# An attention and feed-forward kernel on one core: early subtractions moved from GpSimd to VectorE, a new order of the early stages, and weight loads issued once half 0's x has arrived

## The chip, the core and the metric

The program runs on one core of a Trainium2 chip. The core has TensorE (matmul; PE, its weight loads PEld), VectorE (DVE), ScalarE (ACT), GpSimd (POOL), and SyncE (SP), which here only issues transfers. Each engine works through its own instructions in program order, and engines wait for one another with semaphores. The metric is the device time of one execution in microseconds (us).

## The reference

For 1,024 tokens (32 sequences of 32, 256 features): x is conditioned by a matrix and a bias chosen for each sequence, goes through causal attention with 16 heads, is added back, and then passes a gated layer with low-rank adapters chosen for each sequence, a second gated layer with a Hadamard transform, and a last addition.

```
cond = einsum("bct,bcd->bdt", x, w[subject]) + bias[subject]
q, k, v = split(cond @ W_qkv + b_qkv)
att = softmax(where(causal, q @ k.T / 16, -inf))
x = x + (att @ v) @ W_out + b_out
h = silu(lora(x, Wg, Ag, Bg)) * lora(x, Wu, Au, Bu)
y = lora(h, Wd, Ad, Bd)
x = x + fwht(silu(y @ W1.T) * (y @ W3.T)) @ W2.T
```

## The kernel before

The tokens are handled as two halves of 512 columns, `s` = 0 and 1, and the features in two blocks of 128, `c` or `m` = 0 and 1. To keep float32 precision each operand of a large matmul is a sum of two parts, a hi part (rounded copy, made on ScalarE) and a lo part (the rest, a subtraction), and a product takes three matmuls (hi by hi, lo by hi, hi by lo).

A weight batch `n` of 128 x 512 values is loaded by SyncE into `raw[n % 3]` (`load_weights`), copied on ScalarE into `w_hi` (`split_weights`) and subtracted on GpSimd into `w_lo` (`weights_lo`). So batch n + 3 can be loaded only once `w_lo` of batch n exists. The first batches are W_K = 0, W_Q = 1, W_V = 2, W_OUT = 3, W_GU = 4 and on.

The early stages, in the words of the functions: VectorE picks each slot's conditioning matrix (`condition_product`, `condition_sum`, `condition_blocks`); TensorE multiplies x with it (`conditioned`) and adds the bias (`conditioned_bias`, from a table `fbias` that `condition_bias` makes); ScalarE and VectorE split the result (`conditioned_hi`, `conditioned_lo`). Then come `key` and `query` on TensorE, copied out with a bias by `keys` (half 0: heads 0 and 1 on ScalarE, heads 2 and 3 on VectorE, which waits for ScalarE's) and `queries`; `scores` on TensorE; for each of four score tiles of a half `maxima`, `less_maxima`, `sums`, `inverses` on VectorE, `exps` on ScalarE, `normalised` on GpSimd, `turn` (a transpose) on VectorE, `spread_slots` on ScalarE and `spread_first` on GpSimd; then `v` and `values` on TensorE. The result is gathered by `even_heads` (ScalarE) and `odd_heads` (VectorE) and split by `attention_hi` (ScalarE) and `attention_lo` (VectorE) for the output projection `project`. The residual sum and the gated layers follow.

All orders are written out by hand: each engine's block is a list of calls. SyncE's and ScalarE's transfers go into one queue each, and both queues use the same 16 DMA engines. At the start ScalarE's queue loads the index and x of half 0 (`x_slot[0]`, line 850), SyncE's the constants, three weight batches, x of half 1, `matrix`, `a_in_raw` and `resid` (lines 397 to 435), and then W_OUT and W_GU.

Of the kernel before, what the change touches and what calls it, by code (L numbers as in the profile page):

```python
# [37 lines left out]
ALU = mybir.AluOpType  # L38
# [3 lines left out]
P = 128  # L42
# [64 lines left out]
KEEP_WARM = 4  # L107
# [58 lines left out]
def build(nc, index, first, x_slots, w_stream, matrices, w2_t, x_feat, out):  # L166
    with ExitStack() as ctx:
# [3 lines left out]
        def sem(name):  # L171
            return ctx.enter_context(nc.semaphore(name))
# [106 lines left out]
        w_hi_made = sem("w_hi_made")  # L279
        w_lo_made = sem("w_lo_made")  # L280
# [115 lines left out]
        def _(sp):  # L396
# [33 lines left out]
            for n in range(STAGES):  # L430
                load_weights(n)
# [44 lines left out]
        def _(pe):  # L476
# [66 lines left out]
            def projected(name, n, s, m):  # L543
                w = weights(n)
                ps = claim(name, s, m)
                for c in range(DC):
                    wait_conditioned(s, c)
                    last = both([ps], unit(w, m * DC + c), rows(act_hi, act_lo, c, [s]), c == 0, c == DC - 1)
                full(last[0], name, s, m)

# [297 lines left out]
        def _(act):  # L848
# [220 lines left out]
        def _(dve):  # L1069
# [7 lines left out]
            dve.tensor_copy(idx_row, index_i[:, NG:NG + B]).then_inc(setup, 1)  # L1077
# [7 lines left out]
            def batch_onehots():  # L1085
                dve.wait_ge(setup, 2)
                dve.wait_ge(row_made, 2)
                dve.tensor_scalar(onehot_n[0:2 * LO_ROW, :], idx_row[0:2 * LO_ROW], adapter_row[0:2 * LO_ROW, :], None,
                                  ALU.is_equal).then_inc(onehot_n_made, 1)

            def condition_sum(s):
                dve.wait_ge(prod_cond, s + 1)
                dve.tensor_reduce(cond_sel[:, s * GROUPS:(s + 1) * GROUPS], cond_prod[s], AX.X, ALU.add)\
                   .then_inc(sel_made, 1)

# [154 lines left out]
            batch_onehots()  # L1250
# [15 lines left out]
            keys(0, 1, 2, 3)  # L1266
# [100 lines left out]
        def _(pool):  # L1367
            def weights_lo(n):
                at = n % PLACES * COLS
                pool.wait_ge(w_hi_made, n + 1)  # L1370
                pool.tensor_tensor(w_lo[:, at:at + COLS], raw[:, n % STAGES, :], f32(w_hi[:, at:at + COLS]),  # L1371
                                   ALU.subtract).then_inc(w_lo_made, 1)

# [7 lines left out]
                               float(LO_ROW), None, ALU.subtract).then_inc(row_made, 1)  # L1381
            pool.wait_ge(row_made, 2)
            pool.tensor_tensor(k_bias[:, :, :], const[:, B_K:B_K + DC].unsqueeze(2).to_broadcast([P, DC, 4]),
                               four.unsqueeze(1).to_broadcast([P, DC, 4]), ALU.mult).then_inc(k_bias_made, 1)
            pool.wait_ge(k_bias_made, 1)
# [70 lines left out]
            weights_lo(W_GU)  # L1456
# [3 lines left out]
            spread_first(0, 1, 2, 3)  # L1460
            gather_in(1, 3)
# [129 lines left out]
```

## Time and profile before

| | |
|---|---|
| median of 3 runs | 213.04 us (212.9 to 213.07) |
| the profiled execution | 212.89 us, of which its profile spans 211.1 us |
| PE busy | 205.1 us (97%) |
| DVE, ACT, POOL busy | 93.2, 94.6, 110.4 us |
| DMA | 16.70 MB, mean 79 GB/s |

Times in the profile count from the span's start. The 1.8 us between span and time lie outside the profile. PE's busy time is modelled; what an engine waited for stands in brackets in a timeline row.

### The profile page before, as it was taken

The page shows a single profiled execution, that of the slowest core. Times are in us where ns is not written, and L with a number is a line of the kernel's source. Part 1 is how long each engine was busy: PE and PEld are TensorE (multiplying, and loading weights), DVE is VectorE, ACT ScalarE, POOL GpSimd, SP SyncE. Part 2 cuts the span into 40 slices and gives each one's busy share as a digit, 9 for nine tenths or more (in the row PEclk, how much of TensorE's full clock was granted, in tenths as well). Part 3 has the DMA queues.
Part 4 walks back from the last instruction along what each step waited for, and adds up shares of the span by engine and source line. Part 5 has one row for each costly group of instructions (what it writes and reads, how often), then busy time and mean ns, then how long its engine had stood idle before and what let it go on. Part 6 is the DMA issues. An engine that isn't in the chain of part 4 may idle for free.

```text
span 211.1 us, 5890 instructions
## 1 busy us (share of the span) xinstructions
PE 205.1 (97%) x2361; PEld 163.1 (77%) x2362; DVE 93.2 (44%) x166; ACT 94.6 (45%) x165; POOL 110.4 (52%) x126
## 2 busy tenths in 40 slices
PE   7899999899999999999999999999999999999994
PEld 2567788578777878788788788888888888888894
DVE  3786997895549883020220300068822222220211
ACT  3377898576846043261350361314566664420000
POOL 4596787159846040936742449002699999440000
PEclk9999999999999999999999999999999999999999
DMA  6960055725430470031210460201021000000211
GB/s 148 397 216 5 6 154 156 202 56 159 132 102 0 115 212 31 17 98 25 58 29 23 112 248 11 91 0 50 3 51 50 0 3 0 0 0 3 99 50 50
DMA packets 16266, 16.70 MB, mean 79 GB/s; under 512 B 1776, under 2 KB 13040, under 8 KB 15984
## 3 DMA queue, kind: packets, MB, share of 16 engines
q1 hardware_dynamic: 15952, 15.78, 24.3%
q10 hardware_dynamic: 288, 0.54, 1.1%
q8 instruction: 19, 0.31, 0.6%
q14 instruction: 7, 0.06, 0.1%
HBM read 15.27 MB, written 1.05 MB: 77 GB/s over the span
## 4 chain that ended last, share of the span: by engine, by line
PE 89%; DMA 3%; DVE 3%; ACT 2%; POOL 1%; issue 1%; SPq 0%; POOLq 0%; ACTq 0%; DVEq 0%
PE bank L500 25%; PE bank L502 23%; PE bank L504 23%; PE bank L672 8%; DMA raw<-w_stream 3%; PE bank L712 2%; PE bank L589 2%; PE bank L615 2%; POOL w_lo L1371 1%; DVE aux_lo L1174 1%; PE bank L568 1%; ACT aux_hi L924 1%; PE bank L569 1%; PE bank L570 1%; DVE resid L1182 1%
## 5 line engine op out<-in xcount | busy, mean ns | idle before, releaser
L1429 POOL TENSOR_TENSOR h_lo<-tmp_b,h_hi 128x512 fp32r<-128x512 f32 x32 | 42.6, 1352 | 43.5 <-ACT h_hi L938 43.5
L500 PE MATMUL bank<-act_hi,w_hi 128*128 128x512 f32 x144 | 52.9, 403 | 0.4 <-POOL w_lo L1371 0.2
L502 PE MATMUL bank<-act_lo,w_hi 128*128 128x512 f32 x144 | 51.0, 390 | 0.0
L504 PE MATMUL bank<-act_hi,w_lo 128*128 128x512 f32 x144 | 50.9, 390 | 0.0
L1244 DVE TENSOR_TENSOR tmp_b<-bank,tmp_a 128x512 f32<-128x512 f32 x32 | 20.8, 685 | 62.5 <-ACT tmp_a L945 36.4
L1371 POOL TENSOR_TENSOR w_lo<-raw,w_hi 128x512 fp32r<-128x512 f32 x24 | 31.4, 1315 | 23.6 <-ACT w_hi L868 23.6
L500 PEld LDWEIGHTS bank<-act_hi,w_hi 128*128 128x128 f32 x144 | 27.0, 188 | 8.4 <-issue 1.9
L945 ACT ACTIVATE tmp_a<-bank 128x512 f32<-128x512 f32 x32 | 17.3, 592 | 32.6 <-PE bank L672 28.4
L504 PEld LDWEIGHTS bank<-act_hi,w_lo 128*128 128x128 f32 x144 | 27.0, 188 | 5.8
L502 PEld LDWEIGHTS bank<-act_lo,w_hi 128*128 128x128 f32 x144 | 27.1, 188 | 5.1
L938 ACT ACTIVATE h_hi<-tmp_b 128x512 fp32r<-128x512 f32 x32 | 19.7, 632 | 20.2 <-DVE tmp_b L1244 20.2
L500 PE MATMUL bank<-h_hi,w_hi 128*128 128x512 f32 (+1 forms) x72 | 22.8, 371 | 0.0
L502 PE MATMUL bank<-h_lo,w_hi 128*128 128x512 f32 (+1 forms) x72 | 22.5, 366 | 0.0
L504 PE MATMUL bank<-h_hi,w_lo 128*128 128x512 f32 (+1 forms) x72 | 22.4, 366 | 0.0
L868 ACT ACTIVATE w_hi<-raw 128x512 fp32r<-128x512 f32 x24 | 14.4, 619 | 7.7 <-DMA raw<-w_stream 7.7
L672 PE MATMUL bank<-z_slots,b_own 64*64 64x128 f32 x512 | 15.8, 272 | 0.0
L502 PEld LDWEIGHTS bank<-h_lo,w_hi 128*128 128x128 f32 x72 | 13.6, 189 | 2.3
L504 PEld LDWEIGHTS bank<-h_hi,w_lo 128*128 128x128 f32 x72 | 13.6, 189 | 2.2
L500 PEld LDWEIGHTS bank<-h_hi,w_hi 128*128 128x128 f32 x72 | 13.3, 189 | 2.5 <-issue 0.3
L672 PEld LDWEIGHTS bank<-z_slots,b_own 64*64 64x64 f32 x512 | 13.9, 132 | 1.5 <-issue 1.1
L1344 DVE TENSOR_TENSOR act_lo<-bank,act_hi 128x512 fp32r<-128x512 f32 x4 | 2.6, 686 | 19.3 <-ACT act_hi L1055 19.3
L1416 POOL TENSOR_TENSOR prob<-prob,row_inv 128x512 f32<-128x512 f32 x8 | 8.4, 1051 | 5.1 <-DVE row_inv L1157 5.0
(97 smaller groups left out, 245.7 us busy)
## 6 DMA issues: line engine op xcount, KB each, us to landing
raw<-w_stream SPq DMA_DIRECT2D x24, 256.0 KB, 4.1
b_own<-w_stream SPq DMA_DIRECT2D x32, 128.0 KB, 3.0
resid<-x_feat SPq DMA_DIRECT2D x1, 1024.0 KB, 9.0
tmp_a<-w_t SPq DMA_DIRECT2D x1, 1024.0 KB, 5.1
out_feat<-tmp_b SPq DMA_DIRECT2D x3, 256.0 KB, 2.1
k_x<-x_slots ACTq DMA_DIRECT2D x1, 512.0 KB, 5.1
k_x<-x_slots SPq DMA_DIRECT2D x1, 512.0 KB, 7.2
a_down_raw<-w_stream SPq DMA_DIRECT2D x1, 512.0 KB, 4.0
```

What stands on the lines that cost most here:

```text
L500: pe.matmul(ps[:, :], w[0], x_hi, start=start, stop=False)
L502: pe.matmul(ps[:, :], w[0], x_lo, start=False, stop=False)
L504: last.append(pe.matmul(ps[:, :], w[1], x_hi, start=False, stop=stop))
L589: last = pe.matmul(tiles[i][32 * j:32 * j + 32, g * 4 * T:(g + 1) * 4 * T], q_t[s][q, c, b * T:(b + 1) * T], k_x[s][q, c, b], start=False, ...
L672: ins = pe.matmul(tile(name, s, m)[features, at:at + P], weight(name, s, m, rows_, q)[:, features], slots(name, s, rows_, q).rearrange("p ...
L868: act.activation(w_hi[:, at:at + COLS], raw[:, n % STAGES, :], ACT.Copy)\
L938: act.activation(dst, tmp_b[:, ORDINAL[name, s, m] % 4, :], ACT.Copy).then_inc(prod_hi_made, 1)
L945: free(act.activation(tmp_a[:, n % 4, :], tile(name, s, m)[:, :], ACT.Silu), name, s, m)
L1244: free(dve.tensor_tensor(tmp_b[:, ORDINAL[name, s, m] % 4, :], tile(name, s, m)[:, :], tmp_a[:, silus % 4, :], ALU.mult), name, s, m)
L1371: pool.tensor_tensor(w_lo[:, at:at + COLS], raw[:, n % STAGES, :], f32(w_hi[:, at:at + COLS]), ALU.subtract).then_inc(w_lo_made, 1)
L1416: pool.tensor_tensor(prob[s][:, i], prob[s][:, i], row_inv[:, s, i, :].unsqueeze(2) .to_broadcast([P, 16, T]), ALU.mult).then_inc(normed, 1)
L1429: pool.tensor_tensor(lo, tmp_b[:, n % 4, :], f32(hi), ALU.subtract).then_inc(prod_split, 1)
```

## The change

- `weights_lo` of W_K and W_Q, and `condition_bias(0)`, move from GpSimd to VectorE; `condition_product(1)`, the row of indices and `onehot_n` move from VectorE to GpSimd.
- TensorE drops four filler matmuls (KEEP_WARM), and its first key and query have functions that wait for the lo parts only where each is read. `key(0, 1)` now stands ahead of half 1's conditioning, and `scores(0, 1)` ahead of `key(1, 1)`.
- ScalarE does `keys(0, 1, 0, 1)` ahead of `conditioned_hi(1, ...)`, VectorE does `keys(0, 1, 2, 3)` ahead of `conditioned_lo(1, ...)`.
- GpSimd does `weights_lo(W_GU)` behind half 0's last `spread_first`.
- SyncE issues only W_K at once. It waits until half 0's x has arrived, and then issues W_Q, W_V and all that was behind them.

```
-KEEP_WARM = 4
@@ block.sync
-            for n in range(STAGES):
-                load_weights(n)
+            load_weights(W_K)
+            sp.wait_ge(x_loaded[0], 16)
+            load_weights(W_Q)
+            load_weights(W_V)
             sp.dma_start(x_slot[1], x_slots[:, GROUPS:2 * GROUPS, :]).then_inc(x_loaded[1], 16)
@@ block.tensor
+            def first_key(s, m):
+                ps = claim("k", s, m)
+                for c in range(DC):
+                    at = slice(W_K % PLACES * COLS + (m * DC + c) * P, W_K % PLACES * COLS + (m * DC + c + 1) * P)
+                    wait_read(pe, "xc", s, c)
+                    if c == 0:
+                        pe.wait_ge(w_hi_made, W_K + 1)
+                    pe.matmul(ps[:, :], w_hi[:, at], act_hi[:, c, half(s)], start=c == 0, stop=False)
+                    if c == 0:
+                        pe.wait_ge(w_lo_made, W_K + 1)
+                    pe.matmul(ps[:, :], w_lo[:, at], act_hi[:, c, half(s)], start=False, stop=False)
+                    wait_read(pe, "xd", s, c)
+                    last = pe.matmul(ps[:, :], w_hi[:, at], act_lo[:, c, half(s)], start=False, stop=c == DC - 1)
+                full(last, "k", s, m)
+            def first_query(s, m):
...
+                pe.wait_ge(w_hi_made, W_Q + 1)
...
+                pe.wait_ge(w_lo_made, W_Q + 1)
...
-            for _ in range(KEEP_WARM):
-                pe.matmul(tile("k", 0, 0)[:, :], warm[:, 0:P], warm[:, :], start=True, stop=True)
-            key(0, 0)
-            query(0, 0)
+            first_key(0, 0)
+            first_query(0, 0)
+            key(0, 1)
             conditioned(1, 0)
             conditioned(1, 1)
             conditioned_bias(1, 0)
             conditioned_bias(1, 1)
-            key(0, 1)
             scores(0, 0)
+            query(0, 1)
             key(1, 0)
-            query(0, 1)
+            scores(0, 1)
             key(1, 1)
-            scores(0, 1)
@@ block.scalar
             split_weights(W_OUT)
+            keys(0, 1, 0, 1)
             conditioned_hi(1, 0)
             conditioned_hi(1, 1)
             split_weights(W_GU)
-            keys(0, 1, 0, 1)
+            queries(0, 1)
             exps(0, 0)
             keys(1, 0, 0, 1)
-            queries(0, 1)
@@ block.vector
-            batch_onehots()
             condition_product(0)
             condition_sum(0)
             condition_blocks(0)
-            condition_product(1)
+            condition_bias(0)
+            weights_lo(W_K)
             conditioned_lo(0, 0)
             conditioned_lo(0, 1)
-            identity_rows()
+            weights_lo(W_Q)
             condition_sum(1)
             condition_blocks(1)
+            identity_rows()
+            keys(0, 0, 2, 3)
             row_masks()
-            keys(0, 0, 2, 3)
+            keys(0, 1, 2, 3)
             conditioned_lo(1, 0)
             conditioned_lo(1, 1)
             maxima(0, 0)
             less_maxima(0, 0)
-            keys(0, 1, 2, 3)
             sums(0, 0)
@@ block.gpsimd
-            pool.wait_ge(index_loaded, 16)
-            condition_bias(0)
-            pool.wait_ge(blk_made, 1)
-            weights_lo(W_K)
-            weights_lo(W_Q)
+            pool.wait_ge(w_lo_made, W_K + 1)
+            condition_product(1)
+            pool.wait_ge(fbias_made, 1)
             condition_bias(1)
...
-            weights_lo(W_GU)
             normalised(0, 1)
             spread_first(0, 0)
             normalised(0, 2, 3)
             spread_first(0, 1, 2, 3)
+            weights_lo(W_GU)
             gather_in(1, 3)
             normalised(1, 0)
```

SyncE's first transfers before, with what each waits for (`raw` is a weight batch, `k_x` from `x_slots` is half 1's x):

```order
1 L397 DMA const<-first 128x350
2 L398 DMA fs_rows<-first 8x32
3 L404 DMA raw<-w_stream 128x512 x3
4 L432 DMA k_x<-x_slots 128x1024
7 L435 DMA resid<-x_feat 128x2048
8 L404 DMA raw<-w_stream 128x512 [waits w_lo_made,index_loaded]
```

and in the changed kernel:

```order
3 L404 DMA raw<-w_stream 128x512
4 L404 DMA raw<-w_stream 128x512 [waits x_loaded0]
5 L404 DMA raw<-w_stream 128x512
6 L434 DMA k_x<-x_slots 128x1024
9 L437 DMA resid<-x_feat 128x2048
10 L404 DMA raw<-w_stream 128x512 [waits w_lo_made,index_loaded]
```

The wait stands ahead of the second weight batch, and everything down to W_OUT's load (row 10) is queued behind it.

ScalarE's early instructions before (row 12 is the hi part of W_OUT, row 13 half 1's `conditioned_hi`, row 15 `keys(0, 1, 0, 1)`):

```order
11 L856 ACTIVATE ident_bf<-ident_rows 128x128
12 L868 ACTIVATE w_hi<-raw 128x512
13 L874 ACTIVATE act_hi<-bank 128x512 x2
14 L868 ACTIVATE w_hi<-raw 128x512
15 L889 ACTIVATE k_x<-bank,k_bias,const 128x16x32 x2
16 L905 ACTIVATE prob<-prob 128x512
```

and in the changed kernel:

```order
11 L884 ACTIVATE ident_bf<-ident_rows 128x128
12 L896 ACTIVATE w_hi<-raw 128x512
13 L917 ACTIVATE k_x<-bank,k_bias,const 128x16x32 x2
14 L902 ACTIVATE act_hi<-bank 128x512 x2
15 L896 ACTIVATE w_hi<-raw 128x512
16 L910 ACTIVATE q_t<-bank,const 128x512
17 L933 ACTIVATE prob<-prob 128x512
```

W_OUT's hi part keeps its place; the two key copies now come directly behind it, ahead of half 1's hi parts.

VectorE's instructions before, from half 1's blocks to the first row sums (`k_x` from `bank` are the `keys`, `act_lo` is `conditioned_lo`):

```order
12 L1099 TENSOR_TENSOR prob<-cond_sel,const 128x256
15 L1132 TENSOR_SCALAR k_x<-bank,const,k_bias 128x16x32 x2
16 L1109 TENSOR_TENSOR act_lo<-bank,act_hi 128x512 x2
17 L1140 TENSOR_REDUCE row_max<-bank 128x16
18 L1146 TENSOR_TENSOR prob<-bank,row_max 128x512
19 L1132 TENSOR_SCALAR k_x<-bank,const,k_bias 128x16x32 x2
20 L1152 TENSOR_REDUCE row_sum<-prob 128x16
```

and in the changed kernel:

```order
11 L1134 TENSOR_TENSOR prob<-cond_sel,const 128x256
13 L1167 TENSOR_SCALAR k_x<-bank,const,k_bias 128x16x32 x2
16 L1167 TENSOR_SCALAR k_x<-bank,const,k_bias 128x16x32 x2
17 L1144 TENSOR_TENSOR act_lo<-bank,act_hi 128x512 x2
18 L1175 TENSOR_REDUCE row_max<-bank 128x16
19 L1181 TENSOR_TENSOR prob<-bank,row_max 128x512
20 L1187 TENSOR_REDUCE row_sum<-prob 128x16
```

The second pair of key copies moved from between `less_maxima(0, 0)` and `sums(0, 0)` to ahead of half 1's lo parts.

## Rows read from the trace of the kernel before

**Rows 1.** The page's head, and the granted clock in 40 slices.

```profile
span 211.1 us, 5890 instructions
...
PEclk9999999999999999999999999999999999999999
```

**Rows 2.** The chain that ended last: start us, us, what.

```profile
33.31 1.05 PE bank L615 x60
34.38 0.84 ACT q_t L918 x2
...
36.62 1.58 DVE aux_lo L1174
...
40.73 0.47 PE bank L500
```

**Rows 3.** DMA issues by size: KB each, median us from issue to landing.

```profile
k_x<-x_slots ACTq DMA_DIRECT2D x1, 512.0 KB, 5.1
...
a_down_raw<-w_stream SPq DMA_DIRECT2D x1, 512.0 KB, 4.0
```

**Rows 4.** Landing of L404's loads issued at 2.0, 9.8, 130.4 and 131.7 us.

```profile
L404 SPq DMA_DIRECT2D raw<-w_stream x1: 427/427/427, 2.0 to 2.0; - x1
DMA to landing us min/median/max: 6.2/6.2/6.2
...
L404 SPq DMA_DIRECT2D raw<-w_stream x1: 327/327/327, 9.8 to 9.8; - x1
DMA to landing us min/median/max: 4.6/4.6/4.6
...
DMA to landing us min/median/max: 2.7/2.7/2.7
...
DMA to landing us min/median/max: 5.0/5.0/5.0
```

**Rows 5.** Timeline: start us, us, engine, line, operation, [idle before <-releaser].

```profile
1.19 0.46 ACTq L850 DMA_DIRECT2D k_x<-x_slots  x1
...
12.55 0.99 DVE L1099 TENSOR_TENSOR prob<-cond_sel,const 128x256 f32<-128x256 f32 x1
...
14.99 0.62 ACT L868 ACTIVATE w_hi<-raw 128x512 fp32r<-128x512 f32 x1
...
16.94 1.29 DVE L1109 TENSOR_TENSOR act_lo<-bank,act_hi 128x512 fp32r<-128x512 f32 x2 [1.65 <-ACT act_hi L874]
...
17.66 1.43 ACT L889 ACTIVATE k_x<-bank,k_bias,const 128x512 f32<-128x512 f32 x2
...
19.43 0.69 DVE L1146 TENSOR_TENSOR prob<-bank,row_max 128x512 f32<-128x512 f32 x1
20.04 1.52 DVE L1132 TENSOR_SCALAR k_x<-bank,const,k_bias 128x512 f32<-128x512 f32 x2
20.15 0.63 ACT L905 ACTIVATE prob<-prob 128x512 f32<-128x512 f32 x1 [1.07 <-DVE prob L1146]
...
21.48 0.68 DVE L1152 TENSOR_REDUCE row_sum<-prob 128x16 f32<-128x512 f32 x1
```

**Rows 6.** Timeline of half 0's softmax, the same columns.

```profile
25.62 0.68 DVE L1146 TENSOR_TENSOR prob<-bank,row_max 128x512 f32<-128x512 f32 x1
...
26.65 0.62 ACT L905 ACTIVATE prob<-prob 128x512 f32<-128x512 f32 x1
...
33.05 0.75 ACT L911 ACTIVATE k_x<-k_x,const 128x512 f32<-128x512 f32 x1
```

**Rows 7.** Timeline of GpSimd and VectorE around the attention split.

```profile
24.94 1.31 POOL L1371 TENSOR_TENSOR w_lo<-raw,w_hi 128x512 fp32r<-128x512 f32 x1
...
31.23 1.04 POOL L1422 TENSOR_TENSOR k_x<-k_x,const 128x512 f32<-128x512 f32 x1
...
36.61 1.05 POOL L1416 TENSOR_TENSOR prob<-prob,row_inv 128x512 f32<-128x512 f32 x1 [0.98 <-DVE row_inv L1157]
...
39.84 0.75 DVE L1174 SCALAR_TENSOR_TENSOR aux_lo<-q_t,const,aux_hi 128x512 fp32r<-128x512 f32 x1 [0.25 <-ACT aux_hi L924]
```

More of the change, by code:

```diff
@@ L279, in build @@
         w_hi_made = sem("w_hi_made")
+        idx_row_made = sem("idx_row_made")
         w_lo_made = sem("w_lo_made")
@@ L549, in projected @@
                 full(last[0], name, s, m)
+            def first_key(s, m):
[13 more added lines that the diff above has]
+            def first_query(s, m):
+                ps = claim("q", s, m)
+                at = [slice(W_Q % PLACES * COLS + (m * DC + c) * P, W_Q % PLACES * COLS + (m * DC + c + 1) * P)
+                      for c in range(DC)]
+                pe.wait_ge(w_hi_made, W_Q + 1)
+                for c in range(DC):
+                    pe.matmul(ps[:, :], w_hi[:, at[c]], act_hi[:, c, half(s)], start=c == 0, stop=False)
+                    pe.matmul(ps[:, :], w_hi[:, at[c]], act_lo[:, c, half(s)], start=False, stop=False)
+                pe.wait_ge(w_lo_made, W_Q + 1)
+                for c in range(DC):
+                    last = pe.matmul(ps[:, :], w_lo[:, at[c]], act_hi[:, c, half(s)], start=False, stop=c == DC - 1)
+                full(last, "q", s, m)
             def query(s, m):
@@ L1094, in condition_sum, with condition_bias, weights_lo @@
                    .then_inc(sel_made, 1)
+            def condition_bias(s):
+                b = slice(s * BH, (s + 1) * BH)
+                dve.wait_ge(onehot_n_made, 1)
+                dve.wait_ge(fs_split, 4)
+                dve.tensor_tensor(fbias[:, b], onehot_n[0:BIAS_ROWS, b].unsqueeze(2).to_broadcast([BIAS_ROWS, BH, T]),
+                                  f32(fs_both[:, :]).unsqueeze(1).to_broadcast([BIAS_ROWS, BH, T]), ALU.mult)\
+                   .then_inc(fbias_made, 1)
+            def weights_lo(n):
+                at = n % PLACES * COLS
+                dve.wait_ge(w_hi_made, n + 1)
+                dve.tensor_tensor(w_lo[:, at:at + COLS], raw[:, n % STAGES, :], f32(w_hi[:, at:at + COLS]),
+                                  ALU.subtract).then_inc(w_lo_made, 1)
             def condition_blocks(s):
@@ L1369, in weights_lo @@
                 at = n % PLACES * COLS
+                pool.wait_ge(w_lo_made, n)
                 pool.wait_ge(w_hi_made, n + 1)
@@ L1372, in weights_lo, with condition_product @@
                                    ALU.subtract).then_inc(w_lo_made, 1)
+            def condition_product(s):
+                pool.wait_ge(index_loaded, 16)
+                pool.wait_ge(setup, 1)
+                pool.wait_ge(const_loaded, 16)
+                pool.tensor_tensor(cond_prod[s], cond_all.unsqueeze(1).to_broadcast([P, GROUPS, T, N]),
+                                   onehot_slot[:, s * GROUPS:(s + 1) * GROUPS, :].unsqueeze(2)
+                                   .to_broadcast([P, GROUPS, T, N]), ALU.mult).then_inc(prod_cond, 1)
             pool.memset(f32(ones[:, :]), 1.0).then_inc(ones_made, 1)
@@ L1381, in _ @@
                                float(LO_ROW), None, ALU.subtract).then_inc(row_made, 1)
+            pool.wait_ge(index_loaded, 16)
             pool.wait_ge(row_made, 2)
-            pool.tensor_tensor(k_bias[:, :, :], const[:, B_K:B_K + DC].unsqueeze(2).to_broadcast([P, DC, 4]),
-                               four.unsqueeze(1).to_broadcast([P, DC, 4]), ALU.mult).then_inc(k_bias_made, 1)
-            pool.wait_ge(k_bias_made, 1)
+            pool.tensor_copy(idx_row, index_i[:, NG:NG + B]).then_inc(idx_row_made, 1)
+            pool.wait_ge(idx_row_made, 1)
+            pool.tensor_scalar(onehot_n[0:2 * LO_ROW, :], idx_row[0:2 * LO_ROW], adapter_row[0:2 * LO_ROW, :], None,
+                               ALU.is_equal).then_inc(onehot_n_made, 1)
+            pool.wait_ge(onehot_n_made, 1)
             pool.tensor_copy(fs_both[0:N, :], const[0:N, C_FSIDE:C_FSIDE + T]).then_inc(fs_split, 1)
@@ L1438, in fold_raw_lo @@
                     pool.tensor_tensor(lo, tmp_a[:, j, :], f32(hi), ALU.subtract).then_inc(w2_raw_split, 1)
[L1440 to L1444 removed]
+            pool.wait_ge(fs_split, 4)
+            pool.tensor_tensor(k_bias[:, :, :], const[:, B_K:B_K + DC].unsqueeze(2).to_broadcast([P, DC, 4]),
+                               four.unsqueeze(1).to_broadcast([P, DC, 4]), ALU.mult).then_inc(k_bias_made, 1)
+            pool.wait_ge(w_lo_made, W_K + 1)
+            condition_product(1)
+            pool.wait_ge(fbias_made, 1)
             condition_bias(1)
```

6 lines of the change are left out of this document (removed).

## The prediction

> **What bounds the kernel now.** I read the chain of waits first. From 44 us on it is TensorE alone, one matmul behind the other, so a microsecond won or lost ahead of that point is one in the end time, and nothing behind it is touched by the change. Ahead of it the chain runs over TensorE until the attention output of half 0 at 33.31 us ends, then over ScalarE (34.38 us) and VectorE's `attention_lo` (36.62 us) to the projection at 40.73 us [rows 2]. So two questions decide: when does ScalarE start `even_heads(0, 0)` (34.38 us now; I call this moment E), and how long is the way from E to the projection (6.35 us now)?
>
> E has two masters now. One is TensorE's `values(0, 0)`, which ends at 34.36 us. The other is ScalarE itself: the timeline shows it without a gap from `exps(0, 2)` at 26.65 us to the end of `spread_slots(0, 3)` at 33.05 + 0.75 = 33.80 us [rows 6]. That is only 0.58 us ahead of E. `exps(0, 2)` needs `less_maxima(0, 2)`, which ends at 25.62 + 0.68 = 26.30 us, 0.35 us earlier; I use 0.3 us of it as slack, since a handover costs some 0.05 us. VectorE's softmax work is in turn packed from `sums(0, 0)` at 21.48 us on, one instruction about every 0.6 us with no wait. So TensorE alone being early gives at most 0.58 us. More needs VectorE's `sums(0, 0)` to come earlier, and if that comes later, the loss goes through.
>
> **The change, part by part.**
>
> The loads. Today x of half 0 is issued at 1.19 us and lands 5.1 us later, at 6.3 us [rows 3, 5]; W_Q is issued at 2.0 us and lands 6.2 us later, at 8.2 us; W_OUT is issued at 9.8 us and lands at 14.4 us [rows 4]. These are one unbroken stream: from W_Q's landing to W_OUT's are 6.2 us, for 2,688 KB. ScalarE reads W_OUT at 14.99 us [rows 5], so it has 0.6 us to spare. In the changed kernel the queue runs empty after W_K, and starts again when x is there. When x lands is unknown: not before a 512 KB load with the queue to itself, 4.0 us [rows 3], so 5.2 us; not after today's 6.3 us. I take 5.7 us, since two smaller loads still run beside it. W_Q then takes between 2.7 us, as a lone weight load at 130.4 us did, and 5.0 us, as another lone one at 131.7 us did [rows 4]. I take 3.3 us, nearer the quick one, for most of the 4.0 us of a lone 512 KB load would go to half of it as well [rows 3]. The rest of the stream follows as before, 6.2 us. So W_OUT lands at L = 5.7 + 0.05 + 3.3 + 6.2 = 15.25 us (bounds: 5.2 + 2.7 gives 14.15 us, 6.3 + 5.0 gives 17.55 us). That is 0.85 us later than today. Half 1's x, `matrix` and `a_in_raw` come later by as much; they lie ahead of `resid` in the stream and are needed at 13 us and later, so I cost them at nothing. If that cover is gone, half 1's conditioning slips by the excess, which ScalarE's wait for W_OUT (below) hides up to about 2 us. `resid` is needed only behind the projection.
>
> The Trainium skill, DMA: Bandwidth & Descriptors, Anatomy of one DMA, gives a transfer a fixed cost of about 2.0 us and then bytes over 436 GB/s; by that estimate the 2.75 MB from W_Q to W_OUT take 2.0 + 6.3 = 8.3 us, and L would be 14.05 us, for which the wait below vanishes (the second case among the rivals). It was fitted to GpSimd's transfers, and the trace's lone 5.0 us load is far above its 2.6 us.
>
> ScalarE. Its order puts W_OUT's hi part ahead of `keys(0, 1, 0, 1)` and of half 1's hi parts. It would be ready for it at about 14.1 us: VectorE's `weights_lo(W_Q)` ends near 11.8 us (estimate: the second `conditioned_lo` some 0.5 us earlier than today, then 0.65 us, and as much again if GpSimd's `condition_product(1)` holds it up), then `condition_sum(1)` (1.2 us), blocks (0.99 us today, of which some 0.65 us are a stall beside GpSimd [rows 5]), `identity_rows` (0.4 us) and ScalarE's own copy. All that the change wins before that moment (the bias table and the two lo parts on VectorE at about 0.7 us instead of 1.05 and 1.3 us on GpSimd, the dropped filler, the first key and query some 1.2 to 1.5 us earlier) ends in this wait of 15.25 - 14.1 = 1.15 us. I cost it at nothing, because the cover is a transfer. This is the step that I think matters most.
>
> From L the way to `sums(0, 0)` is a chain of rows. The hi part's pitch is 0.55 us, `keys(0, 1, 0, 1)` take 1.43 us: L + 2.0. VectorE's `keys(0, 1, 2, 3)` wait for them, now ahead of half 1's lo parts, and take 1.45 us to the next instruction (20.04 to 21.48 us): L + 3.5. The two lo parts take 1.2 us at their pitch (1.29 us with the tail): L + 4.7. Then `maxima(0, 0)`, 0.73 us: L + 5.45. From `less_maxima` to the start of `exps` are 0.72 us (19.43 to 20.15), and `exps` take 0.63 us: `sums(0, 0)` at L + 6.8 [rows 5]. At L = 15.25 this is 22.05 us, against 21.48 us now: VectorE is 0.57 us late, although the keys no longer stand in between. The exponent's wait, which the keys filled before, is now idle.
>
> E. `less_maxima(0, 2)` slips by 0.57 us and `exps(0, 2)` by 0.57 - 0.3 = 0.27 us; ScalarE's packed stretch ends at 33.80 + 0.27 = 34.07 us. GpSimd's `spread_first(0, 1)`, which ends at 31.23 + 1.04 = 32.27 us now [rows 7], slips to 32.84 us; `values(0, 0)` take 1.05 us behind it and end at 33.9 us, for TensorE is there about 0.9 us earlier than today. So E = 34.07 us, 0.31 us earlier. As a rule, E = L + 18.8.
>
> From E to the projection. `attention_lo(0, 0)` takes 1.58 us at 36.62 us, and its twin 0.75 us at 39.84 us. The first began 0.01 us behind GpSimd's `normalised(1, 0)`, 36.61 us, which lasts 1.05 us: it stood still until that one had ended [rows 2, 7]. In the changed kernel `weights_lo(W_GU)`, 1.31 us, stands between GpSimd's last `spread_first` and `normalised(1, 0)`. GpSimd starts that `spread_first` at E, ends it at E + 1.1, and is in `weights_lo(W_GU)` until E + 2.4. `attention_lo(0, 0)` is due at E + 2.25, waits 0.15 us, and ends near E + 3.1 instead of E + 3.8. The next step also needs `even_heads(0, 2)`, which is done at E + 3.15. So 0.6 us are won. That rests on VectorE being served before GpSimd's next short copies; if it is not, the price is back to about 0.
>
> Sum: -0.31 - 0.6 = -0.9 us. The profiled execution took 212.89 us, with a span of 211.1 us [rows 1], and lies 0.15 us below the median of the runs shown; against that median I forecast 213.04 - 0.9, some 212.1 us. In general the change is L - 16.2 us.
>
> **Rivals.** A measurement of this kernel tells about 0.2% (0.43 us) from no change.
>
> The restarted queue is quick. If L is at most 14.1 us, ScalarE does not wait, and the change is 14.1 - 16.2 = -2.1 us: 210.9 us. The lone 2.7 us load and the skill's formula speak for it; against it speaks that x would have to land near 5.2 us as well.
>
> No relief at `attention_lo`. The change is then -0.3 us, 212.7 us, within what can't be told. The same result comes from L between 15.8 and 16.6 us with the relief. For it speaks that the blocking hangs on a few hundredths of a microsecond.
>
> The queue is slow: slower than before. The mechanism is the same wait with its price of 1 us for each us of L. It decides from L = 16.65 us on. With x at 6.3 us and W_Q's load at 4.7 us, L is 17.25 us, and the time 214.1 us. The lone 5.0 us load speaks for it, most other loads against it.
>
> A fourth is small: without the filler, TensorE idles some tenths of a microsecond between half 0's bias and the first key. The granted clock is full in every slice today [rows 1], and I know of no gap here longer than the one of 0.6 us ahead of 40.73 us, which cost no clock. I leave it inside the ranges.
>
> **Chances.** Forecast (0.45 to 1.6 us faster) 0.45; quick queue 0.18; no difference 0.22; slower 0.15. So faster 0.63, same 0.22, slower 0.15. The range reaches from the quick queue's 210.8 us to 213.7 us, above which I leave 0.1; the likeliest case alone is 211.4 to 212.6 us.
>
> **What would show it.** ScalarE waits about 1.1 us for a transfer ahead of `w_hi` of W_OUT at 14 to 15 us; if there is no such wait, the loads' step is wrong. VectorE's first `row_sum` starts near 22.05 us, and ScalarE's `even_heads` near 34.05 us. The first `aux_lo` lasts at most 0.95 us; if it still takes 1.5 us, the relief is wrong. The first projection matmul of block 1 stands near 39.8 us, and the stretch behind it has its old length. TensorE's first key ends a microsecond earlier than now without bringing anything. The forecast fails most easily by L, the sum of two landing times that the trace only bounds.

## The result, and the profile after

The change makes the kernel slower: 214.27 us, the median of 7 runs (213.99 to 216.41), against 212.99 us before (212.9 to 213.07). The ratio is 1.0077, with a 95% interval from 1.0045 to 1.0109. Forecast were 212.1 us and a range up to 213.7 us, so the time lies outside of it. Two things are new. The runs spread over 2.4 us where those of before spread over 0.2 us, and five of the seven have a mean granted clock of 0.984 to 0.992 of full speed; the executions of before whose clock is on record have 0.998 or more. The clock does not order the times, though: three of the runs at 0.992 took 213.99, 214.15 and 214.23 us, less than the two at full clock (214.27 and 214.5 us), and the other two took 215.24 and 216.41 us. The profiled execution took 214.27 us with a span of 212.5 us at full clock.

The chain that ended last, of the changed kernel (start us, us, what), answers to [rows 2] at its early end. Before, it left the queue at 7.6 us, ran over ScalarE's and GpSimd's parts of the weights and was TensorE's from 12.3 us on; now it is the queue's until 17.39 us:

```profile
1.19 4.33 DMA k_x<-x_slots
...
5.53 0.33 SPq L404
...
8.35 9.04 DMA raw<-w_stream
...
17.94 1.44 ACT k_x L917 x2
...
19.48 1.53 DVE k_x L1167 x2
21.01 0.61 DVE act_lo L1144
```

W_OUT's load is issued at 8.35 us and lands at 17.39 us, where [rows 4] had 9.8 and 14.4 us. The timeline of the changed kernel (start us, us, engine, line, operation, and what ended the idle time ahead of it) shows what follows, line by line against [rows 5]:

```profile
14.38 3.31 POOL L1456 COPY a_in<-a_in_raw 128x64 f32 x16 [3.50 <-DMA a_in_raw<-w_stream]
...
17.41 0.63 ACT L896 ACTIVATE w_hi<-raw 128x512 fp32r<-128x512 f32 x1 [3.08 <-DMA raw<-w_stream]
...
17.94 1.43 ACT L917 ACTIVATE k_x<-bank,k_bias,const 128x512 f32<-128x512 f32 x2
...
19.48 1.53 DVE L1167 TENSOR_SCALAR k_x<-bank,const,k_bias 128x512 f32<-128x512 f32 x2 [3.77 <-ACT k_x L917]
...
20.93 1.28 DVE L1144 TENSOR_TENSOR act_lo<-bank,act_hi 128x512 fp32r<-128x512 f32 x2
...
23.56 0.63 ACT L933 ACTIVATE prob<-prob 128x512 f32<-128x512 f32 x1 [2.12 <-DVE prob L1181]
```

The reader is to see one wait of 3.08 us on ScalarE for a transfer, and behind it the keys, VectorE's lo parts and the exponent, each at the distance from L that the working gave. Around the attention split, where [rows 6] and [rows 7] stood:

```profile
36.12 0.84 ACT L946 ACTIVATE q_t<-bank,const 128x256 f32<-128x256 f32 x2
...
37.19 1.29 POOL L1408 TENSOR_TENSOR w_lo<-raw,w_hi 128x512 fp32r<-128x512 f32 x1
...
38.36 0.85 DVE L1209 SCALAR_TENSOR_TENSOR aux_lo<-q_t,const,aux_hi 128x512 fp32r<-128x512 f32 x1
...
39.09 1.64 PE L619 MATMUL bank<-k_x,q_t 64*32 64x128 f32 x64
...
42.16 0.42 PE L502 MATMUL bank<-aux_hi,w_hi 128*128 128x512 f32 x1
```

The first `aux_lo` takes 0.85 us instead of 1.58 us, as forecast. E is 36.12 us, and block 1's first projection matmul stands at 42.16 us.

Where the time of the loads went is seen by stretches: us, busy time of PE, PEld, DVE, ACT and POOL, granted clock, share of the DMA engines, GB/s. First before, from 5.5 us on:

```profile
5.50:7.00 1.50, 1.40 (x5) 0.36 (x3) 1.47 (x2) 0.00 (x0) 1.25 (x3) 1.00 1.03 358
7.00:8.50 1.50, 1.01 (x34) 0.85 (x34) 1.50 (x2) 0.63 (x1) 0.28 (x2) 1.00 1.04 416
8.50:11.00 2.50, 2.34 (x41) 1.73 (x41) 1.37 (x3) 1.83 (x4) 1.25 (x2) 1.00 1.08 432
```

Then the changed kernel:

```profile
5.50:7.00 1.50, 1.50 (x5) 0.41 (x3) 1.47 (x3) 0.63 (x1) 0.93 (x4) 1.00 0.34 60
7.00:8.50 1.50, 1.50 (x43) 1.00 (x46) 0.80 (x2) 0.00 (x0) 0.62 (x1) 1.00 0.90 325
8.50:11.00 2.50, 2.50 (x40) 1.54 (x36) 1.49 (x3) 2.03 (x4) 2.38 (x2) 1.00 0.73 177
11.00:14.00 3.00, 3.00 (x13) 2.31 (x13) 2.45 (x5) 2.55 (x5) 0.00 (x0) 1.00 1.03 402
```

Against before, the idle queue costs (358 - 60) x 1.5 = 447 KB, the next stretch 137 KB, and the third (432 - 177) x 2.5 = 638 KB. The third is the one I had not seen coming: the queue is running again and still moves 177 GB/s for 2.5 us. Together they are 1,222 KB, 2.8 us at some 430 GB/s. From 2 to 5.5 us the changed kernel was ahead, 268 against 233 GB/s, which is 0.3 us. That leaves, by this estimate, 2.5 of the 3.0 us by which W_OUT is later; the rest lies in the last packets, which move at 127 GB/s from 16.0 to 16.5 us and at 40 GB/s from then to 17.4 us.

Last, the timeline shows a hole in TensorE's work that before has nowhere:

```profile
16.19 0.92 PE L619 MATMUL bank<-k_x,q_t 64*32 64x128 f32 x46
18.35 0.59 PE L619 MATMUL bank<-k_x,q_t 64*32 64x128 f32 x18 [1.24 <-issue]
...
21.75 0.48 PE L502 MATMUL bank<-act_hi,w_hi 128*128 128x512 f32 x1 [1.22 <-DVE act_lo L1144]
```

Inside `scores(0, 0)`, behind 46 of its 64 matmuls, TensorE stands for 1.24 us and waits for nothing that a semaphore shows. The last row says what this costs here: three microseconds later TensorE waits 1.22 us for VectorE's lo parts, which come late because of W_OUT. Without the hole it would have waited that much longer, so in this execution the late W_OUT covers the hole.

### The profile page after: what moved, and what is told of

The parts are those of the page before. It is cut to its first block, busy times and chain, and to the rows that moved or that the text cites. A ratio compares the mean times of both kernels' runs of the same rounds, so it can differ in the third digit from the quotient of the medians.

```text
span 212.5 us, 5905 instructions
## 1 busy us (share of the span) xinstructions
PE 205.5 (97%) x2358; PEld 162.9 (77%) x2358; DVE 91.9 (43%) x166; ACT 94.6 (45%) x165; POOL 109.8 (52%) x126
## 4 chain that ended last, share of the span: by engine, by line
PE 88%; DMA 6%; DVE 2%; SPq 1%; issue 1%; ACT 1%; ACTq 0%; DVEq 0%
PE bank L502 24%; PE bank L504 22%; PE bank L506 22%; PE bank L702 8%; DMA raw<-w_stream 4%; PE bank L742 2%; PE bank L645 2%; DMA k_x<-x_slots 2%; PE bank L619 2%; PE bank L598 1%; PE bank L674 1%; PE bank L599 1%; PE bank L600 1%; DVE k_x L1167 1%; ACT k_x L917 1%
## 5 line engine op out<-in xcount | busy, mean ns | idle before, releaser
L502 PE MATMUL bank<-act_hi,w_hi 128*128 128x512 f32 x140 | 50.9, 401 | 1.3 <-DVE act_lo L1144 1.2
L504 PE MATMUL bank<-act_lo,w_hi 128*128 128x512 f32 x140 | 49.4, 390 | 0.0
L506 PE MATMUL bank<-act_hi,w_lo 128*128 128x512 f32 x140 | 49.4, 390 | 0.0
L1408 POOL TENSOR_TENSOR w_lo<-raw,w_hi 128x512 fp32r<-128x512 f32 x22 | 28.9, 1313 | 19.9 <-ACT w_hi L896 19.6
L502 PEld LDWEIGHTS bank<-act_hi,w_hi 128*128 128x128 f32 x140 | 26.3, 188 | 8.9 <-issue 1.9
L506 PEld LDWEIGHTS bank<-act_hi,w_lo 128*128 128x128 f32 x140 | 26.3, 188 | 5.7
L504 PEld LDWEIGHTS bank<-act_lo,w_hi 128*128 128x128 f32 x140 | 26.3, 188 | 4.9
L896 ACT ACTIVATE w_hi<-raw 128x512 fp32r<-128x512 f32 x24 | 14.4, 620 | 9.6 <-DMA raw<-w_stream 9.6
```

Of the source, the lines that this page charges most:

```text
L502: pe.matmul(ps[:, :], w[0], x_hi, start=start, stop=False)
L504: pe.matmul(ps[:, :], w[0], x_lo, start=False, stop=False)
L506: last.append(pe.matmul(ps[:, :], w[1], x_hi, start=False, stop=stop))
L896: act.activation(w_hi[:, at:at + COLS], raw[:, n % STAGES, :], ACT.Copy)\
```

## The experiments

All ratios are against the kernel before on the same chip (medians there 212.94 to 213.01 us), with 95% intervals. Times are medians; "profiled" is the one execution whose trace is read.

### The wait alone, away and added

Theory: the wait, by way of W_OUT's landing, is the loss, and the rest of the change is a gain. Rival: the new orders or the move to VectorE lose as well. Taken out of the changed kernel:

```diff
             load_weights(W_K)
-            sp.wait_ge(x_loaded[0], 16)
             load_weights(W_Q)
```

> The changed kernel with SyncE's wait for half 0's x taken out, so that all loads are issued at once as before; all else as changed. Theory (late loads): W_OUT lands near 14.4 us instead of 17.4 us, ScalarE hardly waits for it, even_heads start near 33.0 us instead of 36.1 us, and the time is 3 us below the changed kernel's 214.3 us, 211.2 us. Rival 1 (order of the work: the keys ahead of half 1's parts on ScalarE and VectorE cost the time): 213.5 to 214.3 us. Rival 2 (half 1's x is slow because GpSimd multiplies beside it, not because of the wait): its load still takes near 2.8 us at 170 to 190 GB/s, W_OUT lands near 16 us, and the time is 213 us.

Measured: 211.23 us (211.09 to 211.5), ratio 0.9914 (0.9898 to 0.9931). W_OUT is not waited for, the clock is full in each execution, and `scores(0, 0)` lose at most 0.2 us (1.38 us instead of 1.16). Then the same wait put into the kernel before, with nothing else of the change:

> The kernel before with only SyncE's wait for half 0's x put in ahead of W_Q's load; engines, orders and filler as before. Theory: half 1's x is slow again (4 us from W_V's landing to its own, against 1.4 us), W_OUT lands near 17.4 us, ScalarE waits some 2.4 us for it at 15 us. The keys stand behind it by 2.1 us and VectorE's first row sum comes near 22.4 us, so the time is 0.5 to 1.0 us above before, 213.5 to 214.0 us. Rival 2 (GpSimd's multiplication slows the load): W_OUT lands by 15.9 us and the time is within 0.3 us of before.

Measured: 214.42 us (214.12 to 214.64), ratio 1.0064 (1.0047 to 1.008), 0.4 us above the upper end of what was expected. The two waits that carry it:

```profile
15.39 1.16 PE L527 MATMUL bank<-prob,k_x 64*64 64x64 f32 x64 [1.47 <-DVE prob L1101]
17.29 0.63 ACT L870 ACTIVATE w_hi<-raw 128x512 fp32r<-128x512 f32 x1 [2.25 <-DMA raw<-w_stream]
```

So the change is two changes of opposite sign: the engines' part wins about 1.8 us, and the wait loses it again and 1.3 us more. In the second kernel the same wait costs 1.4 us; ScalarE waits 2.25 us for W_OUT there, 3.08 us in the changed kernel. GpSimd's multiplication for half 1 is not there in the second kernel, and half 1's x lands 3.6 us behind W_V all the same, so it is not what slows the transfer.

### ScalarE does other work first

W_OUT's hi part is moved behind the keys and half 1's hi parts, the wait at SyncE stays:

```diff
-            split_weights(W_OUT)
             keys(0, 1, 0, 1)
             conditioned_hi(1, 0)
             conditioned_hi(1, 1)
+            split_weights(W_OUT)
```

> The changed kernel with one line moved on ScalarE: the hi part of W_OUT comes behind keys(0, 1, 0, 1) and half 1's hi parts, so that these no longer queue behind a late load. The load itself still lands near 17.4 us. Theory (the cost is the place in line, not the load): ScalarE waits behind them instead, VectorE's keys and lo parts come 3 us earlier, its first row sum at 21.5 to 22 us (exps of half 0 now stand behind the wait: 17.4 + 0.55 + 0.55 + 0.7 us is 19.2 us, early enough), and the time is 2 to 3 us below the changed kernel, 211.3 to 212.3 us. Rival (late loads cost elsewhere too, for W_GU or a_in_raw): over 213 us.

Measured: 212.41, 215.88, 214.42 and 215.91 us, at mean clocks of 1.0, 0.984, 0.992 and 0.984; the median of 215.15 us is above the changed kernel's. The profiled one, the first, lies 0.1 us above the upper end of the expectation; the others are far off. So in the one execution at full clock ScalarE's order brings 1.9 us of the 3.0 us that the wait costs. There the rest goes with TensorE's hole (1.49 us here), behind which ScalarE waits 1.89 us for `query(0, 1)`; the other executions lose more, with the clock.

### resid's load behind W_OUT's

```diff
-            sp.dma_start(resid[:, :, :], x_feat).then_inc(resid_loaded, 16)
             sp.wait_ge(index_loaded, 16)
             load_weights(W_OUT)
+            sp.dma_start(resid[:, :, :], x_feat).then_inc(resid_loaded, 16)
```

> The changed kernel with the 1,024 KB load of resid issued behind W_OUT's instead of ahead of it; the wait for x stays. Theory: W_OUT lands 2.5 us earlier, near 14.9 us, ScalarE waits some 0.6 us, and by one us for each us of landing the time is 2.4 us below the changed kernel, 211.9 us. Rival (the slow stretch of half 1's x is what matters and stays): W_OUT still lands after 15.5 us, time 212.4 us or more.

Measured: 212.9 us (212.12 to 215.27, 10 runs), ratio 1.0009 (0.9978 to 1.004). W_OUT costs no wait any more, and still the median is 1.0 us above the expectation: the hole is 1.34 us, and ScalarE waits 2.55 us for the matmuls behind it. The three executions at a clock of 0.992 took 213.62, 214.37 and 215.27 us, the seven others 212.12 to 213.01 us. The late W_OUT and the hole are two costs, and they overlap: the hole has a price where W_OUT is in time, as here, and none in the profiled execution of the changed kernel.

### What slows the restarted queue

Three orders of the loads, to tell a property of the restart (theory R) from one of half 1's x (rival T). First the wait stands behind W_Q's load instead of ahead of it:

> The changed kernel with SyncE's wait for half 0's x moved from ahead of W_Q's load to behind it, so that the queue still has W_Q's 256 KB to move when the wait ends and hardly runs empty. Theory R (a queue that is started again passes, about 1.5 us after its start, through a stretch of some 3 us at 150 to 230 GB/s, whatever is moved): no slow stretch from 8.5 to 11 us, half 1's x lands near 10.5 us, W_OUT near 14.6 us, ScalarE waits at most 0.3 us for it, and the time is 211.2 to 211.8 us. Rival T (half 1's x is slow whenever it is moved beside the engines' work at 8 to 11 us, or behind a wait at all): the stretch stays, W_OUT lands at 16.5 us or later, and the time is 213.5 us or more.

Measured: 212.57 us (212.06 to 213.88, 10 runs), ratio 0.999 (0.9972 to 1.0008). Neither: the queue did not stay busy (172 and 135 GB/s from 6 to 7 us), then moved 343 GB/s for 1.5 us and 176 to 262 GB/s from 8.5 to 10.5 us; W_OUT landed near 15.6 us and ScalarE waited 1.88 us for it.

Then the wait is for half 1's x, behind its load:

> The changed kernel without its wait, and with another one in its place: SyncE waits for half 1's x behind that load's issue, so that the queue runs empty once x is there and starts again with matrix, a_in_raw, resid and W_OUT (1,664 KB). Half 1's x should land near 9.7 us, as in the kernel without a wait. Theory R (the slow stretch belongs to a queue's start): the rate is high for about 1.5 us from the restart, at 150 to 230 GB/s for some 3 us from then (about 13 to 15.5 us), and W_OUT lands near 17.5 to 18 us. Rival T (the slowness belongs to half 1's x or to the time from 8 to 11 us): no such stretch behind the restart, and W_OUT lands near 16.2 us, 2 us of start and 1,664 KB at 430 GB/s behind 9.7 us + 0.05. The time is some 214.5 us by R, some 213 us by T.

Measured: 215.02 and 215.66 us. W_OUT is waited for until 18.28 us, later than both figures. Half 1's x had landed by 9.7 us, and the restarted queue moved on:

```profile
9.50:11.00 1.50, 1.50 (x7) 0.84 (x7) 1.36 (x2) 1.17 (x4) 1.50 (x2) 1.00 0.09 29
11.00:13.00 2.00, 2.00 (x10) 1.65 (x9) 1.97 (x5) 2.00 (x4) 1.08 (x1) 1.00 0.98 280
13.00:16.00 3.00, 3.00 (x98) 2.19 (x104) 1.75 (x5) 0.41 (x3) 2.16 (x12) 1.00 1.01 399
```

For 2 us it is at 280 GB/s, not at 430 and not at 177. Theory R had the slow stretch at 13 to 15.5 us, where 399 GB/s were moved, so it fails here too. Last, half 1's x moved behind `matrix` and `a_in_raw`:

```diff
-            sp.dma_start(x_slot[1], x_slots[:, GROUPS:2 * GROUPS, :]).then_inc(x_loaded[1], 16)
             sp.dma_start(matrix[:, :], matrices).then_inc(matrix_loaded, 16)
             sp.dma_start(a_in_raw.rearrange(...), ...).then_inc(a_in_raw_loaded, 16)
+            sp.dma_start(x_slot[1], x_slots[:, GROUPS:2 * GROUPS, :]).then_inc(x_loaded[1], 16)
```

> The changed kernel, its wait kept, with half 1's x loaded behind matrix and a_in_raw (384 KB) instead of ahead of them. Theory R (the slow stretch belongs to the restarted queue and begins some 1.5 to 2 us behind its restart): from 8.5 to 11 us the rate is 150 to 230 GB/s again, though matrix and a_in_raw are what is moved first, and W_OUT lands near 17.4 us as before. Rival T (half 1's x is what moves slowly): the rate stays above 300 GB/s until about 9.5 us, and is low for some 2.5 us from then. The time says little, since half 1's conditioning waits for its x in either case: 214 to 216 us.

Measured: 213.57 us (213.24 to 213.97), below the 214 to 216 us expected, and W_OUT waited for until 16.82 us instead of 17.4.

```profile
7.00:8.50 1.50, 1.50 (x60) 1.21 (x52) 0.80 (x2) 0.59 (x1) 0.62 (x1) 1.00 0.98 355
8.50:10.00 1.50, 1.50 (x7) 0.94 (x7) 1.10 (x2) 1.05 (x4) 1.50 (x2) 1.00 0.75 202
10.00:11.00 1.00, 1.00 (x5) 0.58 (x4) 1.00 (x2) 0.66 (x3) 0.88 (x1) 1.00 0.84 289
```

The slow stretch begins at 8.5 us again, with other data in it, so it doesn't belong to half 1's x, which is what rival T said. But it is shorter (202, then 289 GB/s), so what stands in the queue has a share in its length. Nor does it belong to what the engines do at that time: in the kernel without the wait 435 GB/s are moved from 8.5 to 11 us. In the orders that restart near 5.5 us R holds for the start of the stretch and not for its size; behind the restart at 10 us it holds for neither. Why a restarted queue passes through it is not shown by any of these.

### resid's load taken out of the stream

First to a place far behind, after `b_own`'s first loads:

> The changed kernel, its wait kept, with resid's load (1,024 KB) issued far later, behind b_own's first loads at about 27 us, so that SyncE's queue is empty from about 14.5 us on. W_OUT should land near 13.5 us and cost no wait. Theory Q (TensorE's hole of 1.2 to 1.5 us inside scores(0,0), with nothing to wait for, is its instructions' transfer standing behind resid's data): no hole, and the granted clock full in all executions; the time is 210.9 to 211.5 us. Theory D (the transfer of the instructions takes its 2.4 us in any case, and TensorE runs into it because half 1's conditioning and scores(0,0) follow each other more densely once half 1's x is late): the hole stays, near 1.3 us, ends some 2.45 us behind the packet of instructions, some executions show a granted clock below 1.0, and the time is 212 to 213 us.

Measured: 212.82, 214.54, 215.85 and 217.34 us. The profiled execution (212.82) has no hole in the scores, as theory Q said. But I had put the load too far back: `b_own`'s sixteen issues hold SyncE until 35.45 us, and VectorE's residual at 41.69 us waits 2.37 us for the data, so TensorE stands 2.09 us there. The other executions show clocks of 0.992 and 0.984. The time therefore says nothing on Q, the trace does. So the place was changed to one that the waits leave free:

```diff
+            wait_full(sp, "s", 0, 0)
+            sp.dma_start(resid[:, :, :], x_feat).then_inc(resid_loaded, 16)
             wait_full(sp, "s", 0, TILES_S - 1)
```

> The changed kernel, its wait kept, with resid's load issued once scores(0, 0) are there (about 17.4 us) instead of at 7.8 us. It should land near 22 us, long before its use at 40 us. Theory Q (the hole in scores(0, 0) is TensorE's next instructions arriving late behind resid's data; its length is the lateness of their packet behind the start of half 1's conditioning, less some 0.45 us): no hole, W_OUT costs at most 0.3 us of wait, the granted clock is full in nearly all executions, and the time is 210.6 to 211.2 us, below the kernel without a wait. Rival (the queue's restart alone loses the clock in some executions, whatever resid does): executions at a mean clock of 0.984 to 0.992 remain, and the median is 212 us or more.

Measured: 211.31 us (210.58 to 211.73, 6 runs), ratio 0.9923 (0.991 to 0.9937), full clock in all six. The median is 0.1 us above the upper end that theory Q gave. With the wait of the change kept, the loss is gone. Its profiled execution has W_OUT at 13.86 us and the whole of `scores(0, 0)` in one piece:

```profile
13.86 0.63 ACT L897 ACTIVATE w_hi<-raw 128x512 fp32r<-128x512 f32 x1 [0.20 <-DMA raw<-w_stream]
...
15.66 1.16 PE L620 MATMUL bank<-k_x,q_t 64*32 64x128 f32 x64
```

The same without the wait:

> The kernel without SyncE's wait, with resid's load issued at the same late place (about 17.4 us). W_OUT was not waited for and there was no hole without the wait, so nothing is left to win: the time should be that without the wait, 211.0 to 211.4 us. With the run before it this tells what the wait itself is worth once both its costs are gone: 0.2 to 0.5 us, because x of half 0 and W_K land up to a microsecond earlier with it. Rival: the wait is worth nothing, and the two are within 0.1 us of each other.

Measured: 211.29 us (210.86 to 211.36), ratio 0.9911 (0.9897 to 0.9924). The rival holds by the medians: with both its costs gone, the wait is worth nothing that shows. Its best execution is 0.3 us below the best without it, its worst 0.4 us above.

### The hole and the instructions' transfer

The page lists packets of a queue called "instruction". Narrow windows give the moment of the one that moves between 13 and 16 us. Beside it stand when TensorE starts half 1's conditioning (two steps ahead of the scores), when it has done 46 matmuls of `scores(0, 0)`, and when it goes on with the 47th, all in us and from the traces:

```
kernel                          conditioning  packet   46 done   goes on   behind packet
resid at 17 us, with wait          13.59       13.7     16.6     at once        -
resid at 35 us, with wait          14.11       14.1     17.1     at once        -
no wait                            14.32       14.8     17.3     0.2 lost       -
resid at 17 us, no wait            14.18       14.8     17.2     0.2 lost       -
no wait, w_lo(W_GU) back           13.94       14.7     16.9      17.17        2.4
wait behind W_Q                    13.60       14.7     16.6      17.31        2.6
half 1's x behind a_in_raw         13.69       15.6     16.7      17.92        2.4
resid behind W_OUT                 13.55       15.5     16.5      17.88        2.4
changed kernel                     14.12       15.8     17.1      18.35        2.5
W_OUT's hi part later              13.58       15.7     16.6      18.07        2.4
wait behind half 1's x             13.57       16.0     16.6      18.41        2.4
```

In all seven kernels with a hole TensorE goes on 2.4 to 2.6 us behind the packet, whatever the hole's length; where the packet comes 2.9 us ahead of need, there is none. (In before's order more work stands in between, and its packet at 15.0 us is in time.) And the packet itself comes the later behind the start of the conditioning, the longer SyncE's queue goes on moving data: 0 to 0.1 us where the queue is at its last packets by then (the first two kernels), 0.5 to 0.8 us where a load is under way until 14 to 14.5 us (the three without the wait), 1.1 us where it moves until 15 us (the wait behind W_Q), and 1.7 to 2.4 us where it moves until 15.5 to 16.5 us (the last five). That is how the wait reaches TensorE: not by data that it needs, but by the stream being busy when TensorE's next instructions are due. What asks for the packet is in no trace; this rests on the eleven kernels' times, and on the hole going with `resid`'s load.

What the hole does to the clock is in the execution in which the profiler caught it, that of the wait behind half 1's x (granted clock is the third figure from the end):

```profile
17.00:18.00 1.00, 0.00 (x0) 0.00 (x0) 0.00 (x0) 0.00 (x0) 1.00 (x1) 1.00 0.06 13
18.00:19.00 1.00, 0.58 (x17) 0.51 (x17) 0.00 (x0) 0.72 (x2) 0.90 (x5) 0.68 0.05 19
19.00:20.00 1.00, 1.00 (x11) 0.55 (x3) 0.00 (x0) 1.00 (x2) 0.94 (x1) 0.50 0.00 0
20.00:21.00 1.00, 1.00 (x4) 0.81 (x3) 0.65 (x1) 1.00 (x3) 0.33 (x1) 0.50 0.00 0
21.00:22.00 1.00, 1.00 (x3) 0.46 (x2) 1.00 (x3) 0.74 (x2) 0.00 (x0) 0.61 0.00 0
22.00:23.00 1.00, 0.48 (x3) 0.36 (x3) 1.00 (x3) 0.69 (x1) 0.00 (x0) 1.00 0.00 0
```

TensorE stood for 1.85 us, and was then granted 0.50 of full speed (the 1.2 GHz level) for 3.4 us. Half speed for 3.4 of 213 us is a mean of 0.992; that is the clock that four executions of the changed kernel list, and 0.984 is twice that loss. That those executions lost it behind the same hole is inferred: their traces were not taken. Here it cost nothing: W_OUT's hi part starts 0.87 us later than in the changed kernel's profiled execution and the time is 0.75 us longer, for behind the slow stretch TensorE still waits 0.52 us for VectorE's lo parts. It has a price where W_OUT is in time, as in the run with `resid` behind W_OUT.

### GpSimd's w_lo of W_GU back at its old place

In the kernel without the wait, `weights_lo(W_GU)` stands again between `gather_in(1, 2)` and `normalised(0, 1)`:

> The changed kernel without SyncE's wait (211.23 us) and with GpSimd's first weights_lo(W_GU) back where it stood before the change, between gather_in(1, 2) and normalised(0, 1). Theory: that move is what gave attention_lo(0, 0) its relief. Then its first aux_lo takes 1.5 us again and not 0.79 us, the first projection matmul of block 1 stands 0.3 to 0.6 us later, and the time is 211.5 to 211.9 us. Rival: the short aux_lo comes from the other orders; then it stays near 0.8 us, and the time stays at 211.1 to 211.4 us.

Measured: 211.45 us (211.14 to 211.96), ratio 0.9926 (0.9912 to 0.9941); without the move 211.23 us. The trace decides it, and for the theory:

```profile
35.69 1.59 DVE L1207 SCALAR_TENSOR_TENSOR aux_lo<-q_t,const,aux_hi 128x512 fp32r<-128x512 f32 x1
...
39.81 0.47 PE L500 MATMUL bank<-aux_hi,w_hi 128*128 128x512 f32 x1 [0.63 <-DVE aux_lo L1207]
```

The first `aux_lo` is at 1.59 us again (0.79 us with the move), and block 1's projection stands at 39.81 us against 39.31 us, with E at 33.45 and 33.47 us. The relief is 0.5 us in the trace; the medians differ by 0.2 us, which the spread of the executions does not tell from nothing.

### The wait in the kernel before, with resid late

> The kernel before with the wait (as in the run of the wait alone, 214.42 us) and with resid's load issued once scores(0, 0) are there. W_OUT's load then lands near 14 us and is no longer waited for; half 1's x and matrix still come late (12.5 to 13.5 us), and in the order of before half 1's conditioning stands right behind the queries, ahead of half 0's last keys. Theory X (with that order the lateness of half 1's x costs by itself): TensorE still waits some 1.4 us at half 1's conditioning, VectorE's act_lo of half 1 start near 18.4 us instead of 18.93 us, and the time is 213.7 to 214.2 us. Rival W (the late W_OUT was all that the wait cost): 212.8 to 213.3 us, that of before.

Measured: 213.66 us (213.48 to 213.92), ratio 1.0031 (1.0018 to 1.0044). Nearer theory X than its rival, but just below X's range: W_OUT is there in time, and TensorE waits 0.58 us (1.4 us expected) at half 1's conditioning, for VectorE was held up 1.43 us by `matrix`. With before's order the late loads ahead of W_OUT cost 0.7 us by themselves; in the changed order, in which VectorE's `identity_rows` (the user of `matrix`) comes behind half 1's blocks and TensorE has one more key to do ahead of half 1's conditioning, they cost nothing (211.31 us with the wait, 211.29 us without it).

## Why the prediction was wrong

**The step that failed** is the last term of L: "The rest of the stream follows as before, 6.2 us". It was 9.3 us, from W_Q's landing at 8.1 us to W_OUT's at 17.39 us. The terms ahead of it were too long, if anything: x landed at 5.52 us (5.7 forecast), and W_Q took 2.6 us (3.3 forecast). The 6.2 us held for a stream that had been running at 358 GB/s and more; I moved the stream's start and kept the rate of its middle. The trace of before could have warned me: its stream too starts slowly, at 233 GB/s from 2 to 5.5 us, and the changed one moves 177 GB/s from 8.5 to 11 us, 3 us behind its second start. The bounds had the same fault. They varied the two landings and left the 6.2 us fixed, so that their end of 17.55 us held the measured value only by accident, and I gave the rival that came true a chance of 0.15. Two readings beside it were wrong and changed nothing. The 2,688 KB are those from W_Q to W_OUT with W_Q's own 256 KB; behind its landing there are 2,432 KB. And the load at 131.7 us, my slow bound for W_Q, was no lone one: it was issued while the one from 130.4 us, which landed at 133.1 us, was still on its way.

**The estimate by the page** failed by more. The Trainium skill, DMA: Bandwidth & Descriptors, Anatomy of one DMA, gave L = 14.05 us, and the measurement decides against its use for a stream that starts anew.

**From L to the projection** every step held. ScalarE was ready for W_OUT at 14.3 us (14.1 forecast) and all that was won ahead of it ended in the wait. `sums(0, 0)` started at 24.22 us (L + 6.8 is 24.19). E = L + 18.8 gives 36.19 us, and 36.12 was measured; the execution with resid at 17 us has L near 13.85 and E at 32.57 us, where the rule gives 32.65. "The change is L - 16.2" gives 1.2 us, and 1.28 us was measured between the medians. It also fits the other kernels in which ScalarE waits for W_OUT in the changed order: W_OUT until 15.63, 16.82 and 18.28 us gives 212.5, 213.7 and 215.1 us on top of 213.04 us, and 212.57, 213.57 us (medians) and 215.02 us (profiled) were measured. So the whole loss of the changed kernel's median is accounted for by W_OUT, with nothing left for the hole. The mechanism was right, and one size in it was not.

**The relief** at `attention_lo` was there with its price: 0.5 us by the experiment, 0.6 forecast. The changed kernel keeps 0.3 of it (from E 6.04 us instead of 6.35), since `scores(1, 1)` in between takes 1.64 us instead of 1.16; the chain names part of that "issue".

**Half 1's x, matrix and a_in_raw at nothing**: right in the changed order, wrong in before's (0.7 us, the last experiment).

**The fourth rival**, the clock, I looked for in the wrong place. The missing filler cost nothing (full clock without the wait). The clock was lost, most likely, behind a hole that the forecast did not have, in five of the changed kernel's seven executions. Its median does not show that loss, for the two executions at full clock took 214.27 and 214.5 us; what made two of them 1.0 and 2.1 us longer than the median stays open.

**The quick queue** was the right picture of the kernel that has no wait: 211.23 us, where I had worked out 210.9 for an L that ScalarE doesn't wait for.

## What to carry to other kernels

Before a stream of loads is made to wait, work out when its last load that anybody waits for would land, with the rate of a starting stream and not of a running one; a load that nobody needs for a long time (here resid, 1 MB, needed at 40 us) must not stand ahead of one that is needed next. A busy queue also went with late instructions for TensorE (by up to 2.4 us here), so a stretch of many short matmuls should not meet the end of a stream. And where a kernel's executions suddenly spread while each is at its own mean clock, look for an idle stretch of TensorE first.

## What was unexpected

**A hole for instructions.** TensorE stood up to 1.85 us in the middle of one `scores`, behind a packet of its instructions that came up to 2.4 us late. The Trainium skill, Runtime: NRT & Kernel Launch, Instruction fetch mechanics, says that the next block is fetched by the sequencer's own queue while the current one runs, and that crossing a block's boundary is mostly hidden. Here it is hidden in some orders and costs 0.2 to 1.85 us in the others; the measurement decides, and what tells them apart is how long SyncE's queue goes on moving data when the packet is due.

**The start of a stream.** A stream does not run at one rate: 233 GB/s in the first 3.5 us of before, 416 to 432 GB/s later; behind a restart 177 GB/s (changed kernel), 202 (half 1's x moved back), 280 (the restart at 10 us). No run shows why.

**The port that VectorE and GpSimd share.** The Trainium skill, SBUF — State Buffer, SBUF: two separate sides, says that of a VectorE instruction with two SBUF inputs and a GpSimd instruction that reads SBUF the one that starts first keeps the shared pair for its whole length. The trace agrees for the first `aux_lo` (1.58 us beside a GpSimd instruction that started 0.01 us ahead of it, 0.85 us in the changed kernel) and at a second place: half 1's blocks on VectorE took 0.99 us in [rows 5], beside GpSimd, and take 0.42 us in the changed kernel, where GpSimd has nothing to do there.
